# Expert tiles of 128 rows, two to a dispatched step, and a finer split of the last sums, in a four-layer transformer kernel

## What is computed

```python
h = layernorm(x) * gamma + beta
top_v, top_i = top_k(softmax(h @ router.T), 2)
gates = softmax(top_v)
out = swiglu(h, shared)
for e in range(8):                          # d_ff 384 for each expert
    y = (silu(h @ gate_e) * (h @ up_e)) @ down_e
    out += gates[e if chosen else 0] * y
x = x + tanh(g_ffn[1]) * out
```

## Time and profile before

| | us |
|---|---|
| median of 3 runs (lowest, highest) | 321.99 (320.24, 324.29) |
| the profiled execution, its own time | 319.61 |
| its span in the trace | 317.8 |
| PE, DVE, ACT, POOL busy | 268.3, 236.4, 204.4, 158.9 |
| mean granted TensorE clock | 0.941 |

### The profile page before, as it was taken

One profiled execution on the slowest core, in us unless ns is written; L12 is line 12 of the kernel. 1 busy time (PEld: TensorE's weight loads), 2 busy tenths in 40 slices (PEclk: granted clock), 3 DMA queues, 4 the chain that ended last, 5 costly groups with the idle time before them and its releaser, 6 DMA issues.

```text
span 317.8 us, 7526 instructions
## 1 busy us (share of the span) xinstructions
PE 268.3 (84%) x2406; PEld 201.9 (64%) x2406; DVE 236.4 (74%) x711; ACT 204.4 (64%) x469; POOL 158.9 (50%) x206
## 2 busy tenths in 40 slices
PE   7878986997999797999988853878899999999950
PEld 4553442555677464676766732368799999999940
DVE  3586198857977666788999967998576767677796
ACT  2964799796577588976855543535657575756560
POOL 2624297024622546643024777770047878787531
PEclk9999999899999999999999655879999999999995
DMA  7890003001269999970000011113122223111064
GB/s 211 233 383 10 1 2 132 0 3 19 117 188 185 178 181 180 190 105 0 2 1 24 30 45 40 53 49 88 37 71 68 78 67 87 51 32 33 8 226 132
DMA packets 34612, 28.12 MB, mean 88 GB/s; under 512 B 3072, under 2 KB 32389, under 8 KB 33936
## 3 DMA queue, kind: packets, MB, share of 16 engines
q1 hardware_dynamic: 32192, 23.77, 33.8%
q0 software_dynamic: 2240, 3.72, 3.6%
q10 hardware_dynamic: 144, 0.15, 0.2%
HBM read 14.15 MB, written 14.40 MB: 90 GB/s over the span
## 4 chain that ended last, share of the span: by engine, by line
PE 52%; DVE 30%; ACT 8%; issue 6%; DMA 2%; SPq 1%; POOL 1%; DVEq 0%
PE bank L1195 47%; DVE region_k L912 2%; DVE region_x L1152 2%; DVE top L911 2%; DMA wr<-in 2%; PE bank L1492 1%; DVE bn_raw L870 1%; DVE nm L1001 1%; DVE region_k L1003 1%; DVE x L1141 1%; DVE x L1142 1%; ACT x_hat L540 1%; DVE x L902 1%; PE bank L1419 1%; DVE region_k L969 1%
## 5 line engine op out<-in xcount | busy, mean ns | idle before, releaser
L1177 DVE TENSOR_TENSOR region_k<-region_x,region_k 128x768 f16<-128x768 f32 (+1 forms) x33 | 30.6, 926 | 21.6 <-ACT region_k L714 21.6
L1195 PE MATMUL bank<-w_high,region_k 128*128 (+1 forms) x380 | 37.8, 221 | 6.4 <-DVE x L1171 3.3
L1195 PE MATMUL bank<-w_scaled,w_high 128*128 128x256 f16 x252 | 42.5, 273 | 0.1
L846 POOL DMA_INDIRECT expert_rows<-region_k,slot_dest x22 | 27.1, 1232 | 26.5 <-DVE region_k L1164 19.2
L714 ACT ACTIVATE region_k<-region_x 128x768 f16<-128x768 f32 (+1 forms) x33 | 26.8, 813 | 15.8 <-DVE region_x L1152 13.7
L820 POOL DMA_INDIRECT dispatched_rows<-region_t,slot x28 | 28.8, 1028 | 16.1 <-issue 8.3
L1195 PEld LDWEIGHTS bank<-w_high,region_k 128*128 128x128 f16 x380 | 30.9, 99 | 7.7 <-issue 7.3
L1195 PE MATMUL bank<-w_scaled,w_low 128*128 128x256 f16 x126 | 34.3, 273 | 0.0
L1195 PE MATMUL bank<-w_low,region_k 128*128 (+1 forms) x190 | 34.0, 221 | 0.0
L1152 DVE SCALAR_TENSOR_TENSOR region_x<-bank,region_w 128x768 f32<-128x768 f32 (+1 forms) x33 | 30.4, 920 | 3.2 <-ACT region_w L719 2.2
L1195 PE MATMUL bank<-filler 128*128 128x512 f16 x94 | 26.9, 407 | 3.9 <-DVE region_k L912 2.4
(11 more groups left out here) (242 smaller groups left out, 736.1 us busy)
## 6 DMA issues: line engine op xcount, KB each, us to landing
dispatched_rows<-pad_rows SPq DMA_DIRECT2D x8, 1048.0 KB, 18.8
w_scaled<-in SPq DMA_DIRECT2D x5, 1024.0 KB, 8.0
w_scaled<-dispatched_rows SPq DMA_DIRECT2D x21, 131.0 KB, 2.3
region_q<-expert_rows SPq DMA_DIRECT2D x3, 512.0 KB, 5.0
x<-in SPq DMA_DIRECT2D x4, 256.0 KB, 4.4
region_w<-in SPq DMA_DIRECT2D x2, 512.0 KB, 7.0
out<-x SPq DMA_DIRECT2D x3, 256.0 KB, 2.3
w_scaled<-in SPq DMA_DIRECT2D x1, 704.0 KB, 4.1
```

Source lines behind the costliest of these rows:

```text
L846: pool.indirect_dma_start(ytok, bass.IndirectOffsetOnAxis(dst[:, n, h:h + 1].bitcast(U32), 0), yv[n % 4][:, h * D:(h + 1) * D], None, boun ...
L1177: dve.tensor_tensor(hsplit[:, v, k:2 * k], hid[:, v, 0:k], hsplit[:, v, 0:k], ALU.subtract).then_inc(hidden_low, 1)
L1195: return pe.matmul(o, l, r, start=start, stop=stop)
```

## The change

- Tiles of 128 rows: `HALVES = (2*14*128 + 8*127) // 128 = 35`, two of them to a step, so `TILES = 18` rows steps and 30 steps in all. Each half has its own expert.
- `gate_up` of a rows step is 6 blocks x 2 halves x 3 matmuls of 128 columns, each half with the weights of its own expert; `down` has as many matmuls as before, but each half its own weights. Shared and dense steps compute as before.
- The tables have 40 entries in place of 32 (`TTAB`), and a window word holds 8 halves, 4 steps, as before without the overlap that `windows_packed` copied.
- SP loads each half with its own DMA behind its own read of the row number (the first four are read ahead); `slot_dest` is two instructions.
- The token rows come in seven pieces. DVE sums tiles 0-5 (none of them inside the last step any more), ACT and POOL tiles 8-13 and 6-7, in pairs of tiles. Six stores in place of five.

```diff
-TILES = (2 * NS * P + E * (TP - 1)) // TP
+HALVES = (2 * NS * P + E * (P - 1)) // P
+TILES = -(-HALVES // 2)
 ROUNDS = -(-TILES // 4)
-TTAB = 4 * ROUNDS + 8
+TTAB = 8 * ROUNDS
+PARTS = ((0, 2), (8, 10), (2, 4), (10, 12), (12, 14), (4, 6), (6, 8))
+BY_DVE, BY_POOL = (0, 2, 5), (1, 3, 4, 6)
+OUT_PARTS = ((0, 4), (8, 12), (NS, NT), (12, NS), (4, 6), (6, 8))
...
-                row = rows[n] if n < AHEAD else eng.value_load(trow_i[0:1, n:n + 1], min_val=0, max_val=E * REG)
-                eng.dma_start(xd[:, n % 4, :, :], disp[ds(row, TP), :].rearrange("(h p) w -> p h w", p=P)).then_inc(rows_loaded[n % 4], 16)
+                for i in (2 * n, 2 * n + 1):
+                    row = rows[i] if i < 2 * AHEAD else eng.value_load(trow_i[0:1, i:i + 1], min_val=0, max_val=E * REG)
+                    eng.dma_start(xd[:, n % 4, i % 2, :], disp[ds(row, P), :]).then_inc(rows_loaded[n % 4], 16)
...
-            for g in (0, 2, 1, 3):
-                n = slice(*GROUPS[g])
-                eng.dma_start(yk[:, n, :], ytok_v[:, n, :]).then_inc(x_loaded[g], 16)
+            for i, (lo, hi) in enumerate(PARTS):
+                eng.dma_start(yk[:, lo:hi, :], ytok_v[:, lo:hi, :]).then_inc(part_loaded[i], 16)
...
+            for k, i in enumerate(BY_POOL):
+                n = slice(*PARTS[i])
                 pool.wait_ge(last_gated, k + 1)
+                for c in range(2):
+                    if c == 1:
+                        pool.wait_ge(last_added, 2 * k + 1)
+                    pool.tensor_tensor(x[:, n, :], x[:, n, :], yk[:, n, c * D:(c + 1) * D], ALU.add).then_inc(last_added, 1)
...
-            def sum_rows(tiles_of_group):
+            def sum_part(i):
+                dve.wait_ge(part_loaded[i], 16)
+                for t in range(*PARTS[i]):
...
-                if s == len(STEPS) - 1:
-                    dve.wait_ge(x_loaded[0], 32)
-                    sum_rows(range(0, 1))
-                elif s == len(STEPS):
-                    sum_rows(range(1, 4))
-            dve.wait_ge(x_loaded[1], 32)
-            sum_rows(range(4, 8))
+                if s == len(STEPS):
+                    sum_part(0)
+            for i in BY_DVE[1:]:
+                sum_part(i)
...
             def gate_up(s, expert):
-                    w = [[v[:, ds(expert, 1), i * P:(i + 1) * P].rearrange("p e n -> p (e n)") for v in gu_w] for i in range(NF)]
-                    xa, xb = xdt[:, s % 2, 0:TP], xdt[:, s % 2, TP:2 * TP]
+                    parts = [([[v[:, ds(expert[h], 1), i * P:(i + 1) * P].rearrange("p e n -> p (e n)") for v in gu_w] for i in range(NF)],
+                              [xdt[:, s % 2, k * TP + h * P:k * TP + (h + 1) * P] for k in range(2)]) for h in range(2)]
...
-                for i in range(len(w)):
-                    o = psum[:, gate_up_bank(s) * 512 + i * m:gate_up_bank(s) * 512 + (i + 1) * m]
-                    mm(o, w[i][0], xa, True, False)
-                    mm(o, w[i][0], xb, False, False)
-                    last = mm(o, w[i][1], xa, False, True)
+                for i in range(count):
+                    for h, (w, (xa, xb)) in enumerate(parts):
+                        c = gate_up_bank(s) * 512 + i * m + h * P
+                        o = psum[:, c:c + m // len(parts)]
+                        mm(o, w[i][0], xa, True, False)
+                        mm(o, w[i][0], xb, False, False)
+                        last = mm(o, w[i][1], xa, False, True)
...
             def down(s, expert):
-                    w = [[v[:, ds(expert, 1), i * D:(i + 1) * D].rearrange("p e n -> p (e n)") for v in dn_w] for i in range(FC)]
+                    of = [[[v[:, ds(expert[h], 1), i * D:(i + 1) * D].rearrange("p e n -> p (e n)") for v in dn_w] for i in range(FC)]
+                          for h in range(2)]
```

More of the change, by code:

```diff
@@ L443, in build @@
         last_added = sem("last_added")
+        part_loaded = [sem(f"part_loaded{i}") for i in range(len(PARTS))]
         def columns(s):
@@ L504, in _ @@
             eng.wait_ge(tiles, 1)
-            rows = [eng.value_load(trow_i[0:1, n:n + 1], min_val=0, max_val=E * REG) for n in range(AHEAD)]
+            rows = [eng.value_load(trow_i[0:1, n:n + 1], min_val=0, max_val=E * REG) for n in range(2 * AHEAD)]
             eng.wait_ge(w_low_done, CHUNKS)
@@ L726, in _ @@
             act.wait_ge(gates_done, 1)
[L727 to L730, removed]
+            for i in BY_POOL:
+                act.wait_ge(part_loaded[i], 16)
+                for t in range(*PARTS[i]):
+                    for c in range(2):
                         last = act.activation(yk[:, t, c * D:(c + 1) * D], yk[:, t, c * D:(c + 1) * D], ACT.Copy,
                                               scale=gate[:, t, c:c + 1])
-                    last.then_inc(last_gated, 1)
+                last.then_inc(last_gated, 1)
         @block.gpsimd
@@ L1093, in windows_packed @@
             def windows_packed():
[L1094 to L1098, removed]
+                link(dve.tensor_scalar(tw[:, :, :], te[:, :].rearrange("p (i j) -> p i j", j=8), float(E - 1), None, ALU.min))
                 link(dve.tensor_tensor(tw[:, :, :], tw[:, :, :],
@@ L1132, in slot_dest @@
             def slot_dest(n):
-                dve.wait_ge(rows_loaded[n % 4], n // 4 * 16 + 16)
-                dve.scalar_tensor_tensor(dst[:, n, :], xd[:, n % 4, :, D + 1], te[:, n:n + 1], xd[:, n % 4, :, D],
-                                         ALU.is_equal, ALU.add).then_inc(dest_ready, 1)
-            def sum_rows(tiles_of_group):
-                for t in tiles_of_group:
+                dve.wait_ge(rows_loaded[n % 4], n // 4 * 32 + 32)
+                for h in range(2):
+                    last = dve.scalar_tensor_tensor(dst[:, n, h:h + 1], xd[:, n % 4, h, D + 1:D + 2], te[:, 2 * n + h:2 * n + h + 1],
+                                                    xd[:, n % 4, h, D:D + 1], ALU.is_equal, ALU.add)
+                last.then_inc(dest_ready, 1)
+            def sum_part(i):
+                dve.wait_ge(part_loaded[i], 16)
+                for t in range(*PARTS[i]):
                     link(dve.scalar_tensor_tensor(x[:, t, :], yk[:, t, 0:D], gate[:, t, 0:1], x[:, t, :], ALU.mult, ALU.add))
@@ L1517, in gate_up @@
                 wait(pe, hidden_done, s - 1)
-                m = xa.shape[1]
-                for i in range(len(w)):
-                    o = psum[:, gate_up_bank(s) * 512 + i * m:gate_up_bank(s) * 512 + (i + 1) * m]
-                    mm(o, w[i][0], xa, True, False)
-                    mm(o, w[i][0], xb, False, False)
-                    last = mm(o, w[i][1], xa, False, True)
-                    if i == (FC if len(w) == NF else 0):
+                m = S if kind == "shared" else TP
+                count = 2 if kind == "shared" else NF
+                for i in range(count):
[5 more added lines that the diff above has]
+                        last = mm(o, w[i][1], xa, False, True)
+                    if i == (FC if count == NF else 0):
                         last.then_inc(gate_made, 1)
@@ L1531, in down @@
                 if kind == "rows":
[L1532 removed]
+                    of = [[[v[:, ds(expert[h], 1), i * D:(i + 1) * D].rearrange("p e n -> p (e n)") for v in dn_w] for i in range(FC)]
+                          for h in range(2)]
                 elif kind == "dense":
[L1534 removed]
+                    of = [[[v[:, n, i * D:(i + 1) * D] for v in dn_w] for i in range(FC)]] * 2
                 else:
[L1536 removed]
+                    of = [[[v[:, W_SD:W_SD + D] for v in (wh, wl)]]] * T
                 pe.wait_ge(hidden_low, s + 1)
                 wait(pe, rows_ready, s)
[L1539 to L1540 removed]
+                m = columns(s) // len(of[0])
+                for h, w in enumerate(of):
                     o = bank[7][:, h * D:(h + 1) * D]
@@ L1557, in expert_of @@
                     return None
-                return e[n % 4] if n // 4 == n_window else before[n % 4]
+                now = e if n // 4 == n_window else before
+                return now[2 * (n % 4):2 * (n % 4) + 2]
             n_window = 0
```

37 lines of the change are left out of this document (14 added, 23 removed).

## The result

| | before | after |
|---|---|---|
| median of 4 runs, us (lowest, highest) | 322.37 (320.24, 324.29) | 350.33 (347.49, 351.02) |
| the profiled execution, its own time | 319.61 | 349.97 |
| its span | 317.8 | 348.2 |
| ratio, with its 95% interval | | 1.0853 (1.076 to 1.0945) |

Slower by 8.5%, where 345 us (331 to 358) was forecast.

What follows compares the result with a forecast made beforehand. TensorE bounds the kernel before; after, its sequencer does, at 0.24 us per addressed pair. As profiled 319.6 + 24.2 (stage) + 0.1 (tables) - 0.2 (end) = 343.7 us; forecast median 345, range 331 to 358.

Steps and rivals of the forecast that it cites:

- The step: Rows step: 18 addressed pairs at 0.24 us plus shifts, masks, waits and transposes' issue, 5.1 us against the engine's 3.19.
- shift and mask 0.43, three waits and the transposes' issue 0.35: Sequencer's work in a rows step besides the addressed pairs: 0.43 us for two experts' numbers, 0.35 us for the rest.
- The stage: First rows gate_up to first dense one behind: from 67.0 us to 90.4, +24.2 with 0.8 added on the pace.
- hitches (0.8): Rows stage: pairs now and then take a little more than 0.24 us; 1% on the pace, 0.8 us.
- Where it starts to hide: Register work in rows steps: hidden from a pair at or below 0.17 us; three matmuls take 0.167 us.
- The matrix engine's own work: TensorE in a rows step: again 3.19 us, two matmuls of 128 columns costing what one of 256 does.
- Tables, SyncE's queue: Larger tables +0.1 us; SP's doubled reads and DMAs, about 2.2 us per step, delay nobody, start taken as 0.
- The end: Summing and storing of token rows: sums done at 314.8 against 315.0 us, -0.2, between -1.5 and +1.0.
- the last store then follows as before: Program's end: the last store comes behind the last sum as in the kernel before, no change.
- Hidden (311): First rival: register work hides as before, rows steps stay 3.19 us, about 311 us in the median; chance 0.07.
- Per matmul (318): Second rival: sequencer paced per 128-column matmul at some 62 ns, step 3.6 us, 318 us; chance 0.04.
- Half clock (357): Third rival: TensorE at half clock in half of the rows steps, 12 us more, 357 us; chance 0.05.

Runs made afterwards that it cites:

- e_before_double: Kernel before with each half of 128 rows addressed for itself from a second register, 18 addressed pairs a step in place of 9; 367.2 us.
- e_before_split: Kernel before with gate_up matmuls of rows steps cut into two of 128 columns, addresses made once for both halves; 324.1 us.
- dose runs: Kernel after with both addresses of a pair made before its first matmul, in gate_up alone 326.3 us, in down alone 336.1 us.
- e_static: Kernel after with rows tiles' weights from fixed expert numbers, so no register instruction for an address between matmuls; 316.8 us, stage 58.0 us.
- e_fuse_stores: Kernel after with fused addresses and seven stores in the order tiles are finished, in place of six; 316.4 us, 0.988 of before.

## Why the prediction was right

**What bounds it: right.** The sequencer was named, at 0.24 us per addressed pair, from two groups of rows of a kernel in which it was hidden; the step of the change shows 18 pairs with ten distances of 0.247 us in `gate_up` (266.24 to 268.71). e_before_double and e_before_split separate it from everything else that was changed.

**The step: a little undersized.** 5.1 us were predicted; the steps are 5.3 apart, 5.7 where a window is loaded. The failing term is "shift and mask 0.43, three waits and the transposes' issue 0.35". From the timeline above: transposes to first group 0.34, to the second 0.54 (the second expert's shift and mask stand here), ten distances 2.47, to `down`'s first 0.35, and from there to the next transposes 1.61. Of these 5.31 us, 18 x 0.24 are 4.32; what is left is 0.99, where 0.78 was put. The stage: 94.2 us against 90.4 + 0.8 = 91.2. The first three distances (4.35, 4.41 and 4.86) are 13.6, where 3.65 + 3.65 + 5.1 + 0.8, less the lead of 0.7, made 12.5. The other 15 steps are 80.6, where 15 x 5.1 with window loads (1.4) and hitches (0.8) made 78.7. Together 3.0 us, 0.17 per step. The split is by the round 0.24; with the 0.247 of `gate_up` for all pairs, 0.13 of the 0.21 us belong to the pairs.

**Where it starts to hide: right.** The prediction had hiding begin for a pair at or below 0.17 us, the work of its own three matmuls. The dose runs show this, and that the sum over a step does not decide. With one instruction to a pair most of the cost is gone; with none, and no shifts and masks, the last 0.19 us per step go too (61.4 less 58.0, over 18).

**The matrix engine's own work: 3.24 us per step, not 3.19.** Two matmuls of 128 columns were taken to cost what one of 256 does; 54 take 3.02 us in e_static and e_before_split, not 2.97. No effect on a kernel bound by its sequencer.

**Tables, SyncE's queue: not contradicted.** +0.1 and 0 were put; nothing above the scatter of the start can be seen. Row loads and their second issue delay nobody: the stage of e_static is as long as its matmuls.

**The end: right sum (-0.2; measured 0.0) by luck, wrong parts.** VectorE was done 343.8 - 318.9 = 24.9 us behind the first dense matmul, before 26.5: 1.6 earlier, where 0.2 was predicted. Sums beside GpSimd took 0.34 to 0.88 us, 0.66 in the mean, where four had been priced at 4.3 us together, 1.07 each. GpSimd's adds are of 256 columns instead of 512; that this is why was not tried. But "the last store then follows as before" failed by as much, 1.6 us. The end of VectorE in the kernel after, and the stretches behind it:

```profile
343.44 0.35 DVE L1146 SCALAR_TENSOR_TENSOR x<-region_q,gates,x 128x128 f32<-128x128 f32 x1
```

```profile
343.20:344.20 1.00, 0.00 (x0) 0.00 (x0) 0.56 (x2) 0.00 (x0) 0.00 (x0) 0.50 1.02 281
344.20:345.20 1.00, 0.00 (x0) 0.00 (x0) 0.00 (x0) 0.00 (x0) 0.00 (x0) 0.50 1.03 287
345.20:346.20 1.00, 0.00 (x0) 0.00 (x0) 0.00 (x0) 0.00 (x0) 0.00 (x0) 0.50 1.04 290
346.20:347.20 1.00, 0.00 (x0) 0.00 (x0) 0.00 (x0) 0.00 (x0) 0.00 (x0) 0.50 0.39 110
347.20:348.20 1.00, 0.00 (x0) 0.00 (x0) 0.00 (x0) 0.00 (x0) 0.00 (x0) 0.50 0.00 0
```

All of x, 1 MB, is stored once VectorE has summed its fourth tile (the first store is issued at 341.98), at 281 to 290 GB/s until 346.6, and then GpSimd's drain holds the end: 4.4 us from the last sum, 2.8 before.

**The sum.** As profiled, 343.7 us were predicted and 349.97 measured, 6.3 more: 3.0 in the stage, 0.2 in the end, and 3.1 because the first rows `gate_up` came 3.2 us later than in the trace of before, where 0.1 was put. The last is the scatter of the start, so half of the miss tells nothing about the change. From profile to median 1.3 us were added (343.7 to 345) and 0.4 was right, which takes 0.9 back: 5.3 above the forecast.

**The rivals.** Hidden (311): what the kernel becomes when one instruction of each pair goes, 316.9. The Trainium skill ("Runtime: NRT & Kernel Launch", "Instruction fetch mechanics") has an issue floor of about 20 cycles per instruction. A floor is no price, and this rival took it for one: among matmuls a plain register instruction costs 0.10 us here, which the floor allows but doesn't give. Per matmul (318): 3.6 us to a step, excluded by e_static's 3.24 with the same matmuls. Half clock (357): the clock was granted in full through all the stage, with matmuls in 3.2 of 5.3 us.

## What to carry to other kernels

When operands are addressed by registers, count the register instructions of each matmul group and hold their pace, read from start to start in the trace of a kernel where they are still hidden, against that group's own matmuls: halving the columns per address can uncover what cost nothing. Make all addresses of a group ahead of its first matmul, so that they fuse; here that turned a loss of 8.5% into a gain of 1%, though whether fewer instructions or their place did it stays open. And before more is given to GpSimd at the end of a program, look at what its sequencer still does behind its last instruction.

## What was not expected of the hardware

- From its last add on, GpSimd's sequencer stands in a DRAIN of 6.1 to 6.7 us, to 5.3 us beyond the add's end (18 rows steps) or 5.8 (21); in the kernel after this is what ends the program. In e_fuse_stores no engine and no transfer is at work in its last 2.0 us.
- A plain register instruction between two matmuls of a group costs 0.10 us though it lasts 32 ns, nearly the same in `gate_up` (22.1 us for 216) and in `down` (10.1 for 108); why is not known. A fused one of 55 ns ahead of the group, which makes both addresses, costs 0.01 us, shifts and masks included (3.4 us for 324).
- TensorE is shown as busy for 88.5 of the stage's 94.2 us, though its matmuls fill 18 x 3.24 = 58; lengths that contain the passage through the array hide gaps of 0.07 us.
